# Two halves or one whole: the products with A of a graph network kernel in float32

## The reference

```python
h = relu(layernorm(x))
msg = (h[src] + edge_attr) @ Wm.T + bm
agg = segment_sum(msg, dst) / max(deg, 1)
out = h + gelu(concat(h, agg) @ Wu.T + bu)
x = x + layernorm(out) * gamma + beta

h = relu(layernorm(x))
rst = (1 + eps) * h + segment_sum(h[src], dst)
x = x + (relu(rst @ W1 + b1) @ W2 + b2 + h)
```

## Time and profile before

| | us |
|---|---|
| median of 3 runs (range) | 487.54 (486.55 to 487.87) |
| profiled execution | 488.46 |
| its span, first to last instruction | 486.7 |
| PE busy in it | 471.4 (97%) |
| DVE, ACT, POOL busy | 266.0, 165.5, 120.6 |
| mean granted clock of PE | 0.996 |

### The profile page before, as it was taken

How to read it: one execution, slowest core, us unless ns; L and a number is a source line. 1 busy time by engine, 2 the same in 40 slices (tenths; PEclk the granted TensorE clock), 3 DMA queues, 4 the chain that set the end, 5 groups by cost and what they waited for, 6 DMA issues and landing times.

```text
span 486.7 us, 9356 instructions
## 1 busy us (share of the span) xinstructions
PE 471.4 (97%) x3297; PEld 281.4 (58%) x3297; DVE 266.0 (55%) x614; ACT 165.5 (34%) x312; POOL 120.6 (25%) x185
## 2 busy tenths in 40 slices
PE   7999999999999999999999999899999999999997
PEld 5545545455545456777766655799744449444442
DVE  4798886778787878876958699923000000011011
ACT  6677642333333338412047287620012213000000
POOL 4016343443344331000001113249980000000000
PEclk9999999999999999989999999999999999999999
DMA  8999999999999999996330111040230000010111
GB/s 283 382 396 408 408 386 373 403 392 406 401 373 393 407 404 398 369 349 237 147 105 23 43 43 40 5 170 1 56 118 0 0 0 1 22 43 23 43 43 38
DMA packets 31720, 98.92 MB, mean 203 GB/s; under 512 B 3672, under 2 KB 4696, under 8 KB 31674
## 3 DMA queue, kind: packets, MB, share of 16 engines
q1 hardware_dynamic: 30458, 97.27, 52.9%
q10 hardware_dynamic: 1216, 1.05, 0.7%
HBM read 95.76 MB, written 2.56 MB: 202 GB/s over the span
## 4 chain that ended last, share of the span: by engine, by line
PE 82%; DVE 8%; issue 4%; DMA 2%; DVEq 1%; POOL 1%; ACT 1%; SPq 0%; POOLq 0%
PE ps L1452 14%; PE ps L1437 14%; PE ps L1170 11%; PE ps L1218 6%; PE ps L1189 6%; PE ps L1384 4%; PE ps L1198 4%; PE ps L1279 4%; PE ps L1360 3%; PE ps L1280 3%; PE ps L1361 3%; PE ps L1122 3%; PE ps L1178 2%; DMA WmN<-in_L_gnn_Wm_dram 1%; DVE acc L790 1%
## 5 line engine op out<-in xcount | busy, mean ns | idle before, releaser
L438 POOL TENSOR_TENSOR aggT<-turned_sums,aggT 128x88 f32 x118 | 61.0, 517 | 97.3 <-ACT turned_sums L511 84.3
L746 DVE TENSOR_TENSOR A<-ps,A 128x220 f32 x158 | 60.7, 384 | 33.1 <-PE ps L1189 24.2
L1088 DVE TENSOR_TENSOR U<-ps,U 128x512 f32<-128x512 f32 (+1 forms) x10 | 6.9, 692 | 128.5 <-PE ps L1452 128.5
L1452 PE MATMUL ps<-W2s,hid 128*128 128x512 f32 (+1 forms) x160 | 68.8, 592 | 0.0
L1437 PE MATMUL ps<-aggT,W1s 128*128 (+1 forms) x192 | 67.3, 513 | 0.0
L1170 PE MATMUL ps<-ea,oneD 128*22 128x256 f32 x944 | 62.6, 383 | 3.2 <-issue 2.2
L1437 PEld LDWEIGHTS ps<-aggT,W1s 128*128 128x128 f32 x192 | 36.4, 190 | 30.7 <-issue 30.6
L1170 PEld LDWEIGHTS ps<-ea,oneD 128*22 128x22 f32 x944 | 23.3, 101 | 50.1 <-issue 26.3
L1452 PEld LDWEIGHTS ps<-W2s,hid 128*128 128x128 f32 (+1 forms) x160 | 30.0, 188 | 38.2 <-issue 38.2
L505 ACT COPY packed_sums<-ps 128x256 f32<-128x256 f32 x59 | 22.0, 372 | 80.9 <-PE ps L1170 80.7
L1360 PE MATMUL ps<-AR,Hh 128*128 128x256 f32 (+2 forms) x160 | 44.0, 311 | 0.7 <-DVE Hl L1055 0.7
(11 more groups left out here) (149 smaller groups left out, 651.8 us busy)
## 6 DMA issues: line engine op xcount, KB each, us to landing
ea<-in_edge_attr_dram SPq DMA_DIRECT2D x78, 1024.0 KB, 8.7
X<-in_x_dram SPq DMA_DIRECT2D x1, 2304.0 KB
xt<-in_x_dram SPq DMA_DIRECT2D x9, 256.0 KB, 3.6
out_dram<-U SPq DMA_DIRECT2D x9, 256.0 KB
W1s<-in_L_gnn_W_dram SPq DMA_DIRECT2D x1, 2048.0 KB, 9.0
W2s<-in_L_gnn_W_dram SPq DMA_DIRECT2D x1, 2048.0 KB, 8.3
Wu2N<-in_L_gnn_Wu_dram ACTq DMA_DIRECT2D x2, 512.0 KB, 4.4
WmN<-in_L_gnn_Wm_dram SPq DMA_DIRECT2D x1, 1024.0 KB, 7.2
```

Of the source, the lines that this page charges most:

```text
L438: nc.gpsimd.tensor_tensor(cols, sums, cols, ALU.add).then_inc(early_step, 1)
L746: V.tensor_tensor(cols, ps[:, 4 + m % 2, half * KW:(half + 1) * KW].rearrange("p (h w) -> p h w", w=W), cols, ALU.add).then_inc(add_step, 1)
L1452: last = T.matmul(ps[0:rows, 6 + b % 2, :], hid[:, k, b * P:b * P + rows], W2s[:, k, :], start=k == 0, stop=k == KC - 1)
```

## The change

The products with A take whole float32 operands: X (h0, later h1) and A converted to float32, one matmul in place of the two with Hh and Hl. The halves, their tiles, the casts and subtractions that made them and their semaphores are gone, as is the path for large counts with its number, loads and branches. The degree products are issued as two halves of five at n = 68 and n = 70. The loop on PE takes every step alone: a group's sums, then one piece. The adds of bu start earlier (n = 62 in place of 67), those of the map's bias later (two a step, from n = 74). POOL's residual adds X once in place of both halves. Tile addresses shift by 1,024 bytes.

```diff
+    DEG_AT = FOLD_AT[-1] + 2
+    DEG_PARTS = [range(0, NT // 2), range(NT // 2, NT)]
+    BIAS_AT = [n for n in range(EARLY + 3, EARLY + NT + 4) if n != OUT_AT]
+    HAS_AT = [NG - (NT - b + 1) // 2 for b in range(NT)]
-    DEG_AT = FOLD_AT[-1] + 3
-    BIAS_AT = [n for n in range(DEG_AT - 2, DEG_AT + NT - 1) if n != OUT_AT]
-    HAS_AT = [min(OUT_AT + 1 + b, NG - (NT - b + 1) // 2) for b in range(NT)]
-    PAIRS_FROM = PIECE_AT + 4
-    PAIRED = [[n] for n in range(PAIRS_FROM)] + [[n for n in (k, k + 1) if n < NG] for k in range(PAIRS_FROM, NG, 2)]
...
-    Hl, _ = place("Hl", [P, NT, D], F32R, x_at)
-    Hh, hh_at = place("Hh", [P, NT, D], F32R)
-    ARc, arc_at = place("ARc", [P, NT, 512], F32R)
-    AR, _ = place("AR", [P, NT, NP], F32R, stream_at)
+    ARc, arc_at = place("ARc", [P, NT, 512], F32)
+    AR, _ = place("AR", [P, NT, NP], F32, stream_at)
...
-            sp.wait_ge(most_ready, 2)
+            sp.wait_ge(deg_mm, 2)
...
-            sp.wait_ge(past_large, 1)
...
-                pool.wait_ge(res_step, b * 3 + 1)
-                nc.gpsimd.tensor_tensor(t, t, Hh[:, bass.ds(b, 1), :].bitcast(F32), ALU.add).then_inc(res_step, 1)
-                pool.wait_ge(res_step, b * 3 + 2)
-                nc.gpsimd.tensor_tensor(t, t, Hl[:, bass.ds(b, 1), :].bitcast(F32), ALU.add).then_inc(res_step, 1)
+                pool.wait_ge(res_step, b * 2 + 1)
+                nc.gpsimd.tensor_tensor(t, t, X[:, bass.ds(b, 1), :], ALU.add).then_inc(res_step, 1)
...
-                nc.scalar.copy(Hh[:, b, :], X[:, b, :]).then_inc(hi0_ready, 1)
-            large = act.value_load(most1[0:1, 0:1], min_val=0, max_val=E + P)
-                nc.scalar.copy(Hh[:, b, :], X[:, b, :]).then_inc(hi1_ready, 1)
...
-                V.tensor_tensor(Hl[:, b, :], X[:, b, :], Hh[:, b, :].bitcast(F32), ALU.subtract).then_inc(low0_ready, 1)
-                dve.wait_ge(deg_mm, 1)
-                V.tensor_reduce(most1_f[0:1, 0:1], ps[0:1, DEG_BANK, 256:256 + P], AX.X, ALU.max).then_inc(most_ready, 1)
+                dve.wait_ge(deg_mm, 2)
-                    V.tensor_reduce(most[:], Dsum[:], AX.X, ALU.max).then_inc(fold_step, 1)
-                if n == DEG_AT:
+                if n == DEG_AT + 4:
                     degrees()
-                V.tensor_tensor(Hl[:, b, :], X[:, b, :], Hh[:, b, :].bitcast(F32), ALU.subtract).then_inc(split1, 1)
...
-            def degree_products():
-                pe.wait_ge(fold_step, HB)
-                T.transpose(ps[0:1, DEG_BANK, 256:256 + P], most[:], ident[:])
-                for d in range(NT):
+            def degree_products(part):
+                pe.wait_ge(fold_step, HB - 1)
+                for d in part:
...
-                    pe.wait_ge(low0_ready, c + 1)
+                    pe.wait_ge(h0_ready, c + 1)
...
-                    T.matmul(to, Hh[:, c, rows], here, start=c == 0 and (q < 2 or f % 2 == 0), stop=False)
-                    last = T.matmul(to, Hl[:, c, rows], here, start=False, stop=c == NT - 1 and (q < 2 or f % 2 == 1))
+                    last = T.matmul(to, X[:, c, rows], here, start=c == 0 and (q < 2 or f % 2 == 0), stop=c == NT - 1 and (q < 2 or f % 2 == 1))
...
-            for pair in PAIRED:
-                for n in pair:
-                    sums(n)
+            for n in range(NG):
+                sums(n)
+                if 0 < n <= EARLY:
+                    turn(n - 1)
+                if n in (DEG_AT, DEG_AT + 2):
+                    degree_products(DEG_PARTS[(n - DEG_AT) // 2])
...
-                for n in pair:
-                    if n >= PIECE_AT:
-                        piece(n - PIECE_AT)
+                if n >= PIECE_AT:
+                    piece(n - PIECE_AT)
...
-                pe.wait_ge(split1, b + 1)
+                pe.wait_ge(h1_ready, b + 1)
...
-                    T.matmul(to, Hh[:, b, rows], AR[:, b, start:start + cols], start=b == 0 and (cols == 512 or f % 2 == 0), stop=False)
-                    last = T.matmul(to, Hl[:, b, rows], AR[:, b, start:start + cols], start=False, stop=b == NT - 1 and (cols == 512 or f % 2 == 1))
+                    last = T.matmul(to, X[:, b, rows], AR[:, b, start:start + cols], start=b == 0 and (cols == 512 or f % 2 == 0),
+                                    stop=b == NT - 1 and (cols == 512 or f % 2 == 1))
```

More of the change, by code:

```diff
@@ L50, in gnn_kernel @@
     LAST = N - QS[-1][0]
-    XW = 256
-    NX = NP // XW
     WU_ORDER = list(range(FC, 2 * FC)) + list(range(FC))
     assert ETAIL % 2 == 0 and ETAIL <= GE // 2 and D == GE and FC == 4 and sum(n for _, n in QS) == NP
-    assert len(QS) == 3 and QS[2][1] * 2 == 512 and KW <= 256 and NT == 10
+    assert len(QS) == 3 and QS[2][1] * 2 == 512 and KW <= 256 and NT == 10 and E < 1 << 16
     EAGER = FC - 1
@@ L108, in place @@
         return nc.alloc_sbuf_tensor_at(name, shape, dt, offset=offset), offset
-    X, x_at = place("X", [P, NT, D], F32)
-    Hl, _ = place("Hl", [P, NT, D], F32R, x_at)
-    Hh, hh_at = place("Hh", [P, NT, D], F32R)
+    X, _ = place("X", [P, NT, D], F32)
+    first_at = at[0]
+    at[0] += (2 * FC + 1) * D * 4 + FC * QUAD * 4 + P * 4
     U, u_at = place("U", [P, NT, D], F32)
@@ L121, in gnn_kernel @@
     Wu1N, _ = place("Wu1N", [P, FC, D], F32, u_at)
[L122 to L126, removed]
+    WmN, _ = place("WmN", [P, FC, D], F32, first_at)
+    Wu2T, _ = place("Wu2T", [P, FC, D], F32, first_at + 8192)
+    bm_parts, _ = place("bm_parts", [P, D], F32, first_at + 16384)
+    bmB, _ = place("bmB", [P, FC, QUAD], F32, first_at + 18432)
+    onesP, _ = place("onesP", [P, P], F32, first_at + 18944)
     acc, _ = place("acc", [P, NP], U16, w1_at)
@@ L139, in gnn_kernel @@
     at[0] = -(-at[0] // 64) * 64
-    ARc, arc_at = place("ARc", [P, NT, 512], F32R)
-    ARd, _ = place("ARd", [P, NT, 256], F32R, arc_at + NT * 256 * 4)
-    AR, _ = place("AR", [P, NT, NP], F32R, stream_at)
+    ARc, arc_at = place("ARc", [P, NT, 512], F32)
+    ARd, _ = place("ARd", [P, NT, 256], F32, arc_at + NT * 256 * 4)
+    AR, _ = place("AR", [P, NT, NP], F32, stream_at)
     hid, _ = place("hid", [P, KC, NP], F32, stream_at)
@@ L643, in _ @@
                     full_conv(k + 2)
-                for work, lag in ((gelu, 0), (h1, 3), (h1_high, 3), (h1T, 3)):
+                for work, lag in ((gelu, 0), (h1, 3), (h1T, 3)):
                     if 0 <= k - lag < NT:
@@ L894, in _ @@
                     bias_out()
-                for b in range(NT):
-                    if HH_AT[b] == n:
-                        low_h0(b)
                 for c in range(1, HB):
@@ L969, in _ @@
             dve.wait_ge(agg_done, 2 * FC)
[L971 to L983, removed]
-                            last = V.tensor_tensor(part, ps[:, CHUNK_BANK[f], 0:XW], part, ALU.add)
-                        last.then_inc(extra_add, 1)
-                        dve.wait_ge(extra_add, q * NT + c + (done + 1))
-            dve.wait_ge(most_ready, 2)
-            large = dve.value_load(most1[0:1, 0:1], min_val=0, max_val=E + P)
-            with dve.If(large > COUNT_MAX):
-                dve.wait_ge(extra_conv, 1)
-                extra(0)
             def packed(first):
@@ L1060, in _ @@
             STEPS = [(update, 0), (center, 2), (add_h0, 1), (add_x, 2), (o_moments, 1), (shift, 3), (x1_moments, 2), (add_beta, 1), (o_moments2, 1),
-                     (x1_moments2, 2), (o_variance, 1), (x1_variance, 2), (low_h1, 4)]
-            for k in range(NT + 5):
+                     (x1_moments2, 2), (o_variance, 1), (x1_variance, 2)]
+            for k in range(NT + 4):
                 if k == 5:
@@ L1080, in _ @@
             dve.wait_ge(rst_done, 4)
-            with dve.If(large > COUNT_MAX):
-                extra(1)
-            V.nop().then_inc(past_large, 1)
             for b in range(NT):
                 dve.wait_ge(y_mm, b + 1)
-                dve.wait_ge(res_step, 3 * b + 3)
+                dve.wait_ge(res_step, 2 * b + 2)
                 rows = P if b < NT - 1 else TAIL
@@ L1328, in _ @@
                         pe.wait_ge(gen_add, NT * GEN)
-                for n in pair:
-                    if n >= PIECE_AT:
-                        piece(n - PIECE_AT)
+                if n >= PIECE_AT:
+                    piece(n - PIECE_AT)
             for i in range(IN_LOOP, 2 * NT):
                 piece(i)
-            def extra(layer):
-                done = layer * NX * NT
-                with pe.Fori(0, NX) as q:
-                    with pe.Fori(0, NT) as c:
-                        pe.wait_ge(extra_ready, q * NT + c + (done + 1))
-                        for f in range(FC):
-                            to, rows = ps[:, CHUNK_BANK[f], 0:XW], slice(f * P, (f + 1) * P)
-                            T.matmul(to, parts[:, 0, rows], rest[:, 0:XW], start=True, stop=False)
-                            last = T.matmul(to, parts[:, 1, rows], rest[:, 0:XW], start=False, stop=True)
-                        last.then_inc(extra_mm, 1)
-                        pe.wait_ge(extra_add, q * NT + c + (done + 1))
```

(11 more changed lines are left out.)

51 lines of the change are left out of this document (1 added, 50 removed).

## The result

The changed kernel takes 560.05 us (median of 4 runs, 559.76 to 560.20), against 487.71 for the kernel before (4 runs): ratio 1.149, 95% interval 1.147 to 1.151, 72.3 us more. The forecast was 557.2, from 553 to 563. The profiled execution took 560.09 us with a span of 558.3, 71.6 more than before.

The account below looks back on a forecast made before the run. PE was taken as the bound, busy 471.4 of 486.7 us. Products +77.0 less 7.3 for waits, clock and switches (stages +28.4, +6.3, +35.0) made +69.7 on 487.54, so 557.2 us, range 553 to 563.

Parts of the forecast that it names:

- the price of a whole product: Products with A: a whole float32 product costs 0.859 us against 0.467 per pair at 512 columns; +77.0 us in all.
- 256 columns, taken from a line through two other shapes: Chunks B and C: 0.437 us per whole product, interpolated between 0.388 at 226 and 0.859 at 512 columns; +16.8 us.
- Nothing hides: All three stretches with the products: none of the +77.0 us has room; idle PE is 0.77, 0 and 3.13 us.
- part of it is hidden: Rival: if type switches were dear, all of 0.33 a step, the second part regains 4 us and more; 553, chance 0.06.
- I book 0 for the unpairing: Piece stage: taking steps singly instead of in pairs costs 0 us, bounds -4.1 and +1.8; a step takes 4.54.
- switches around the transposes: Second part: ten transposes lose the type switch on each side, 5.6 to about 4.2 us; -1.4, bound 0.
- From the profiled execution to the median: Whole run: forecast 558.2 us for the profiled execution, lowered to 557.2 because that execution stood 0.92 above the median.
- The first piece: Start of the piece stage: without halves it no longer waits 0.70 us for DVE's low half; -0.7 us.
- DVE as pacer of the second part: Second part: DVE stops setting the pace, PE's 3.13 us idle closes but for 0.43 before the second transpose; -2.7, bound 0.
- The clock: Piece stage: splitting the degree products leaves no fall of the granted clock; -1.6 us, bound +3.4; falling-again rival chance 0.13.
- Free edits: POOL's low-half adds, value loads and branches, W2's earlier load: no PE cost seen; greatest count's removal also booked at no effect.
- the -0.65 booked for waits for DVE: Piece stage: other PE waits for DVE, of the 0.77 us idle, vanish once a step takes 4.5 us; -0.65.

## Why the prediction was right, point by point

- **What bounds the kernel, and the price of a whole product.** Right. 280 products were priced at +77.0 us by spacing of records; one layer alone gives +36.5 and the other +34.8 (expected of these two runs, without the clock's share: +36.6 and +35.0), and a block of chunk A, eight records of 512 columns, goes by in 3.43 us. That a record's mean duration is no price is shown as well: 592 to 604 ns after against 422 before would have given 1.4 times, the spacing gives 1.84 times.
- **256 columns, taken from a line through two other shapes.** 0.437 was taken. In PE's timeline the blocks of chunk A and B together take 5.16 us, 3.44 of them chunk A's, so 0.43 for one. Right.
- **Nothing hides.** Right for both layers. The rival that part of it is hidden is refuted, for the pieces by a stage without idle PE and for the second layer by +34.8 in place of +27.
- **The steps one by one, "I book 0 for the unpairing".** This is the term that was mis-sized. Restoring the pairs gives 2.5 us back in the changed kernel. I had the 0.33 from the earlier trace rows, but then took an average over the stage of before, which held 0.75 us more than its 4 single steps and 7 pairs explain, and a price for after that left out part of the switch. The plain reading was 1.20 for every single step and 1.04 for one of a pair. The upper bound of the term, a step of 4.64 in place of 4.54, is what came: 1.8 us over the 18 steps, against the 1.6 by which the piece stage outran its forecast. The cheap reading, that the switch is the data type's and goes with it, is refuted there: 4.64 us with float32 on both sides. In the second part 1.4 us were booked for switches around the transposes, and the stage came out within 0.3 of the forecast, but that small term was not tested by itself.
- **From the profiled execution to the median.** The sum took 1.6 us off for the fall of the clock and then another 0.92, because the profiled execution stood that far above the median. But it stood there with its fall, so part of it was taken off twice: from an execution without a fall the same terms give 486.58 + 69.7 + 1.6 = 557.9. That is 0.7 of the 2.85 us by which the forecast was low; the changed kernel's profiled execution (560.09) and its median (560.05) are the same.
- **The first piece.** 0.44 of the 0.7 us came; PE is idle for 0.18 us ahead of it, for which the profile names no releaser. ACT's conversion of A for it ends at 186.96, just before PE is free at 187.04, so it may be what holds it; that is not shown.
- **DVE as pacer of the second part.** Right: PE's idle time there is 0.43 us, before the second transpose and behind ACT's h1, as named:

```profile
320.14 0.66 PE L1254 MATMUL ps<-ident,X 128*128 128x128 f32 x4 [0.43 <-ACT X L584]
```

- **The clock.** No fall in any of the changed kernel's executions, as forecast, and the blocks of five are the reason (no fall in 27 executions of the changed kernel and the three others that have them and no long wait; 16 falls in 37 executions of the five experiments with ten in a row and all else for PE to do, and 35 in 57 of the kernel before). But I treated the 1.6 us as part of the kernel before, when 22 of its 57 executions don't have them. The gain of the cut is 1.6 us in about six of ten executions. The rule weighed in the prediction, the Trainium skill's "TensorE: Matmul & The Clock Gate", HAM oscillation, ties falls to waits without matmuls between bursts. In the kernel with the second layer alone changed the clock fell right behind the ten one-column products with PE busy throughout (9.00 of 9.00 and 4.00 of 4.00 us above), so the traces do not agree that a wait is needed. With the wait of 2.94 us in the kernel with pairs from 60 they do agree that one can bring a fall, and so they do in the kernel without the low half's products, where second sums wait 2.77 us for DVE until 212.58 and the clock is 0.50 from 214.0 to 218.0.
- **"Free edits".** Not quite: the greatest count, which went at no effect, cost 0.7 us, 0.4 of it through DVE by a wait on PE of which the earlier trace rows show the sum only (0.77 idle) and 0.1 by its transpose; 0.2 is open. In the changed kernel the wait is inside the -0.65 booked for waits for DVE. POOL's adds and W2's load changed nothing seen: there is no such wait on PE.

Put together in executions without a fall: 486.6, less 0.7 for the path, plus 36.5, 34.8 and 2.5, is 559.7; the changed kernel has 560.05.

## What to carry to other kernels

Price a matmul by the distance between starts in a dense stretch of the same type and width, times the records that one call leaves. Two records mean nothing by themselves: a pair of float32r halves and a whole float32 product both leave two, and the second costs 1.8 times the first. Where narrow and wide products alternate on PE, count the changes (here 0.33 us for one way in and back) and group them, as far as the operands of the second group are there in time. Before a gain of under 2 us is claimed, look at the granted clock of every execution.

## What was not expected of the hardware

- The same program falls to the lower clock in some executions and not in others: 35 of 57 for the kernel before, 1.6 us between the medians. Six of the 35 have a clock of 0.993 and take 489.39 to 490.11, as two falls would. With the one-column products in blocks of five there was no fall behind them in any of 27 executions; with ten in a row 3 of 5, 5 of 12, 5 of 12, 1 of 4 and 2 of 4 had one. The kernel with a wait of 2.94 us between narrow products had one in 11 of 12.
- The change between narrow products (22 columns of weights side by side) and full ones costs 0.33 us for a way in and out whatever the types. In the kernel before, 0.13 of it lies ahead of the first wide record (1.00 us behind the sums' start, where a second group adds 0.87), 0.10 between the first two wide records and 0.10 behind the last.
- With PE's work cut by 46 us the mean granted clock went down to 0.974 in the profiled execution and 0.981 to 0.982 in the others: less work for PE was answered with a slower PE, and under half of the saving came through.
